# Expert addresses of each run at multiples of 16 numbers in the row that TensorE loads from

## What is computed

```python
x = x + 0.5 * ffn(layernorm(x), gate_w, w1, w3, w2)
x = x + attn(layernorm(x), time_mix_k, ..., Wk, Wv, Wr, Wo)
x = x + 0.5 * ffn(layernorm(x), gate_w, w1, w3, w2)

def ffn(x, gate_w, w1, w3, w2):           # E = 8 experts, top 2, F = 512
    probs = softmax(x @ gate_w)
    expert_weights, expert_indices = top_k(probs, 2)      # then normalised to sum 1
    for i in range(E):
        wi = where(expert_indices == i, expert_weights, 0.0).sum(-1)
        h = silu(x @ w1[i]) * (x @ w3[i])
        out = out + (h @ w2[i]) * wi[..., None]
```

## Time and profile before

| | us |
|---|---|
| median of 3 runs | 621.75 (621.48 to 623.04) |
| profiled execution, its own time | 623.24 |
| its span, first to last instruction | 621.4 |
| TensorE matmuls busy | 521.1 (84%), 5866 instructions |
| TensorE weight loads busy | 477.7 (77%) |
| VectorE busy | 423.8 (68%) |
| GpSimd busy | 389.3 (63%) |
| ScalarE busy | 318.9 (51%) |

### The profile page before, as it was taken

The page is one execution under the profiler, slowest core; times in us unless marked ns, Lnnn a source line. Parts: engine busy times, 40 slices in busy tenths (PEclk is TensorE's granted clock), DMA queues, the critical chain, the costliest instruction groups (busy, mean ns, idle before and its releaser), DMA issues.

```text
span 621.4 us, 18551 instructions
## 1 busy us (share of the span) xinstructions
PE 521.1 (84%) x5866; PEld 477.7 (77%) x5866; DVE 423.8 (68%) x1218; ACT 318.9 (51%) x703; POOL 389.3 (63%) x490
## 2 busy tenths in 40 slices
PE   1235899999999899998999959998989999989930
PEld 1233789898978789877898849887879899978930
DVE  4862863556878988799998955887788765215431
ACT  5433674444585565756676534776473444434410
POOL 1171058489999970599808996003949887835973
PEclk9999899999999999999999979999998999989985
DMA  8963233544232221212221133111121442313332
GB/s 284 329 192 113 61 92 114 156 137 124 79 116 65 78 74 53 74 60 73 78 66 53 59 101 87 49 37 36 54 81 57 121 112 83 103 45 99 91 89 59
DMA packets 89062, 59.55 MB, mean 96 GB/s; under 512 B 10256, under 2 KB 82704, under 8 KB 88976
## 3 DMA queue, kind: packets, MB, share of 16 engines
q1 hardware_dynamic: 55296, 29.97, 16.5%
q0 software_dynamic: 8192, 16.79, 8.9%
q10 hardware_dynamic: 25488, 11.61, 6.5%
HBM read 28.65 MB, written 29.69 MB: 94 GB/s over the span
## 4 chain that ended last, share of the span: by engine, by line
PE 56%; DVE 13%; ACT 11%; issue 8%; POOL 8%; DMA 3%; POOLq 0%; ACTq 0%; DVEq 0%; SPq 0%
PE py L1259 18%; PE pa L1245 14%; PE pb L1245 12%; POOL rows_in L725 3%; ACT xn L817 3%; POOL yg L737 3%; DVE h L1114 3%; PE pT L1232 2%; PE bkB L1318 2%; PE bkB L1297 2%; ACT sil L798 2%; POOL pace L754 2%; PE bkA L1312 2%; ACT rT L778 1%; PE bkA L1297 1%
## 5 line engine op out<-in xcount | busy, mean ns | idle before, releaser
L725 POOL DMA_INDIRECT rows_in<-parts,slot x128 | 135.0, 1054 | 183.1 <-DVE slot L1039 161.2
L1114 DVE TENSOR_TENSOR h<-sil,pb 128x512 f32<-128x512 f32 x177 | 120.7, 686 | 127.3 <-ACT sil L798 79.6
L1259 PE MATMUL py<-ffn_w,h 128*128 x1416 | 198.6, 284 | 9.4 <-ACT yrow L783 9.0
L1259 PEld LDWEIGHTS py<-ffn_w,h 128*128 128x128 f32 x1416 | 175.2, 195 | 15.2 <-issue 12.3
L1245 PE MATMUL pa<-rT,ffn_w 128*128 128x128 f16 (+1 forms) x1752 | 151.7, 233 | 22.8 <-issue 12.5
L1245 PE MATMUL pb<-rT,ffn_w 128*128 128x128 f16 (+1 forms) x1752 | 154.5, 232 | 0.0
L1245 PEld LDWEIGHTS pa<-rT,ffn_w 128*128 x1752 | 124.2, 99 | 37.6 <-issue 26.4
L737 POOL DMA_INDIRECT yg<-rows_out,slot x128 | 125.4, 980 | 38.6 <-issue 22.8
L754 POOL MEMSET pace<- 128x544 uint8 x223 | 127.7, 573 | 0.1
L1245 PEld LDWEIGHTS pb<-rT,ffn_w 128*128 x1752 | 122.2, 98 | 6.8
L798 ACT ACTIVATE sil<-pa 128x512 f32<-128x512 f32 x177 | 105.3, 595 | 40.4 <-PE pa L1245 39.9
(11 more groups left out here) (156 smaller groups left out, 459.2 us busy)
## 6 DMA issues: line engine op xcount, KB each, us to landing
rows_out<-yrow ACTq DMA_DIRECT2D x177, 64.0 KB, 1.9
rin<-rows_in SPq DMA_DIRECT2D x65, 128.0 KB
rows_in<-zrow SPq DMA_DIRECT2D x34, 128.0 KB, 2.0
shared<-in_w SPq DMA_DIRECT2D x16, 256.0 KB, 6.7
rin<-rows_in SPq DMA_DIRECT2D x47, 64.0 KB
rows_in<-zrow SPq DMA_DIRECT2D x2, 1472.0 KB, 11.0
xres<-in_x SPq DMA_DIRECT2D x4, 512.0 KB, 6.3
ffn_w<-in_w SPq DMA_DIRECT2D x8, 256.0 KB, 5.2
```

The lines of the kernel that those rows point to most:

```text
L725: pool.indirect_dma_start(rows_in[g][:], bass.IndirectOffsetOnAxis(ap=slot[:, c, at:at + 1], axis=0), parts[:, at, :], None).then_inc(s_sc ...
L1114: dve.tensor_tensor(h[:, t % RING, :], sil[:, t % 2, :], pb[t % 2][:], ALU.mult).then_inc(s_h, 1)
L1259: mm = pe.matmul(py[:], h[:, step % RING, at:at + T], w, start=(c == 0), stop=(c == FC - 1))
```

## The change

The start of each run's numbers in `eid` is rounded up to a multiple of 16: each run takes a multiple of 16 places, of which it uses `NE[run]`. The two places that sliced up to the next run's start now slice by the count.

```diff
 NE = tuple(STEPS[r] if OPEN[r] or MORE[r] else NQ[r] for r in range(RUNS))
-ESTART = tuple(sum(NE[:r]) for r in range(RUNS + 1))
+LINE = 16
+ESTART = tuple(sum(-(-n // LINE) * LINE for n in NE[:r]) for r in range(RUNS + 1))
...
                 np, n = PAIRS[run], NE[run]
-                te, ids = teid[:, 0:n], eid[:, ESTART[run]:ESTART[run + 1]]
+                te, ids = teid[:, 0:n], eid[:, ESTART[run]:ESTART[run] + n]
...
                 _, found = nc.values_load_multi_w_load_instructions(
-                    eid[0:1, ESTART[run]:ESTART[run + 1]], engines=(mybir.EngineType.PE,), min_val=0,
+                    eid[0:1, ESTART[run]:ESTART[run] + NE[run]], engines=(mybir.EngineType.PE,), min_val=0,
```

## The result

| | us |
|---|---|
| before, median of 6 runs | 622.06 (621.23 to 623.04) |
| after, median of 6 runs | 611.89 (611.39 to 612.55) |
| ratio after / before | 0.9836, 95% interval 0.9823 to 0.9849 |
| span of the profiled execution | 610.1 after, 621.4 before |

The change makes the kernel 10.2 us faster. The forecast was 11.0 us faster, 610.8 us, with a range of 607.5 to 615.

What follows compares the result with a forecast made beforehand. TensorE was taken to bound the kernel, waiting for expert-address loads at three places. Gains of 5.5 + 2.3 + 3.2 = 11.0 us (runs 5, 6, 8) took 621.75 to 610.8 us, eight in ten from 607.5 to 615.

Steps and rivals of the forecast that it cites:

- That the start decides: TensorE's expert-address loads: cheap from starts at a multiple of 16 numbers in eid, about 0.24 us a number from others.
- The loads after: Loads of runs 5, 6 and 8 after the change: 2.4, 0.995 and 1.13 us, from 7.10, 2.198 and 2.87.
- Run 5: forecast 5.5: At run 5's load of thirty numbers: 4.7 us saved by the load plus 0.8 us of clock.
- The clock's half share, 0.8: Behind run 5's new gap of 1.9 us: the middle between nothing (clock falls) and 1.5 us back (clock kept).
- Run 6: forecast 2.3: At run 6's load of nine numbers: 1.2 us of load plus 2.2 behind the gap, 3.4 limited to 2.3 us.
- The cap: Run 6's third tile waits for VectorE's h whatever the load does, limiting that run's gain to 2.3 us.
- Run 8: forecast 3.2: At run 8's load of twelve numbers: 1.74 us saved by the load plus 1.5 us from the clock staying at 2.4 GHz.
- The tail: GpSimd's last gathers: first one near 555 us instead of 565.8, with the same 55.6 us to the end.
- The moved tensors: Tensors allocated behind eid begin 96 bytes later in every partition: taken as 0, within 1 us either way.
- the rival that matmuls pay for them: Tile matmuls slower from the new starts of rT and h; 2.2 ns each loses the whole gain; 3 in 100.
- That the clock falls all the same: Rival: TensorE at half clock behind all three gaps, only the loads' 7.6 us saved, 614.1 us; 16 in 100.
- That a load pays per number wherever it starts: Rival: the start doesn't set a load's price, so nothing changes, 621.7 us; 4 in 100.

Runs made afterwards that it cites:

- e5: Changed kernel with every run's numbers starting one place behind a multiple of 16; 640.9 us beside 622.0 for the kernel before, ratio 1.0304.
- e0: The whole changed kernel measured once more, nothing else altered; 611.64 us beside 622.01 for the kernel before, ratio 0.9838.
- e6: Changed kernel with the nine loads starting at rests 1, 2, 4, 8, 12, 0, 2, 0, 12 after division by 16; 620.83 us beside 623.05 before.
- e7: Changed kernel with the nine loads starting at rests 8, 12, 2, 4, 8, 4, 8, 2, 10 after division by 16; 621.66 us beside 623.05 before.
- e2: Changed kernel in which, of the three dear loads, only run 5's starts at a multiple of 16; ratio to the kernel before 0.9907.
- second e1: Repeat: eid 30 numbers longer as in the changed kernel, all starts as before the change; 635.78 us beside 636.18, ratio 0.9993.
- e4: Changed kernel in which, of the three dear loads, only run 8's starts at a multiple of 16; ratio to the kernel before 0.9954.

## Why the prediction was right, point by point

**What bounds the kernel, and which loads are dear.** Right. The price of a dear load was read as 0.24 us a number from three rows. The runs give 0.24 to 0.25 for 9, 12, 22 and 30 numbers in runs 5 to 8. In runs 0 to 4 a dear number cost more, 0.25 to 0.28 in the loads of sixteen and 0.26 in e5's load of nine; why is open.

**That the start decides.** Right as to the start, too narrow as to which. From the rows of before nothing tells 4 from 16, since their cheap starts (0, 16, 32, 48, 64, 112) are multiples of both; the step "a multiple of 16" was taken from the change, not from rows. The forecast of this kernel didn't suffer.

**The loads after.** Forecast 2.4, 0.995 and 1.13 us, measured 2.520, 0.907 and 0.857. Twelve numbers cost no more than nine.

**Run 5: forecast 5.5, stretch 4.8.** The load's 4.7 came as 4.6. The clock's half share, 0.8, was put in for one fall in two; it fell, for a shorter time than before, and the run's first two tiles took 369.50 - 362.75 = 6.75 us instead of 375.44 - 368.44 = 7.00, so 0.25 came back. That is the term that was too big: of the five traces with this load cheap and in one piece at the run's start, the clock fell in four (after, e0, e6, e7) and was kept in e2 alone, where 7.00 - 5.40 = 1.6 came back, near the 1.5 put down for that case.

**Run 6: forecast 2.3, stretch 1.6.** The cap held to the tenth: the third tile starts 473.83 - 464.3 = 9.5 us after the load's start before, 465.64 - 458.4 = 7.2 after, and waits for h. But the gains behind a gap were mis-sized, which the cap hid. I had the first tile back at 2.29 us with the clock at 2.4 GHz. It takes 462.53 - 459.55 = 2.98, at a granted clock of 1.00. The wait for h is a gap as well, and the tile behind it takes 468.48 - 465.64 = 2.84. The late start of the fourth tile takes back some 0.6 of the 2.3. The clock's part was also less sure than it looked: before the change the same gap of 1.7 us sometimes keeps the clock (second e1, e4), and then the whole run has 0.4 to 0.5 us to give.

**Run 8: forecast 3.2, stretch 3.6.** The load was 0.3 shorter than thought, and the clock stayed, which was worth 1.6 where 1.5 was put down. Its first tile takes 546.10 - 543.89 = 2.21 us, as paired tiles do without a gap; the extra of narrow tiles is not seen here.

**The sum.** Runs 5 and 6 gave 0.7 us less each and run 8 gave 0.4 more, so the errors partly cancel: the total, 10.1 against 11.0, is nearer in proportion than any of its three terms, and that much of it is luck.

**The tail.** Right: it begins 11.25 us earlier, and takes the same time.

**The moved tensors, and the rival that matmuls pay for them.** Forecast 0 within 1 us; measured 0.3 and 0.4 us faster by the ratios, with two intervals that hold zero.

**The other rivals.** That the clock falls all the same came true in run 5 alone. That a load pays per number wherever it starts is false. By the rule of the Trainium skill (Runtime: NRT & Kernel Launch, Instruction fetch mechanics), about 200 ns a register, thirty registers would take an estimated 6 us. The measurement decides: 7.1 us at a start off a multiple of 4 numbers, 2.4 to 2.6 at one on it.

## What to carry to other kernels

When an engine loads registers from SBUF, look at each load's duration beside its count and its start: a start off a multiple of 16 bytes can hide in a table of offsets and cost 0.24 us a number, on the path of that engine. Before hoisting such a load, ask what is queued in front of it: behind six matmuls of 512 columns 1.5 us were hidden whole, behind the same matmuls 2.6 us were not, and behind four small transposes not even 0.86. A gap on TensorE costs more than its length, and the row's releaser is a guess when two things end close together; another kernel's trace can settle it.

## What the runs showed of the hardware that I had not expected

- A load from SBUF into TensorE's registers is cheap (sixteen numbers 1.1 to 1.7 us, thirty 2.4 to 2.6) from any start at a multiple of 16 bytes, and takes 0.24 to 0.28 us a number from any other that was tried (1, 2 or 3 numbers past such a multiple). That one reads several numbers at a time and the other one by one fits these sizes, but was not shown.
- Behind gaps of 0.4 to 1.9 us a tile of narrow matmuls (128 columns) takes 2.8 to 3.0 us instead of 2.3, at a granted clock of 1.00; a tile with 256 columns takes its usual 2.2. That the sequencer has lost its lead over the array is likely, since narrow matmuls leave it the least time for each, but no run isolates it.
- The same gap of 2.4 us behind run 8's load lost the clock in one profiled execution and kept it in another, and that alone moved the stretch from 13.8 to 15.4 us. Over all traces the clock was lost in six and kept in two at this gap of 2.4 to 2.5 us, lost in five and kept in two at run 6's 1.7, and lost in four and kept in one at run 5's 1.9 to 2.05. So a price for the clock is a chance times a cost, in the kernel before as well as in the changed one.

What stays open: why the clock falls behind a gap in one execution and not in the next, why dear numbers cost more in the early runs, and how much of run 6's gain reaches the end, which no interval separates from nothing.
